# A context loop of VectorE written out, and another order of work at the end of a state space stage

## The reference

```python
# stage D, per batch b and head h: keys and values are the rotated context
scores = jnp.einsum('bhsr,bhlr->bhsl', q_r, k_r)
attn   = jax.nn.softmax(scores, axis=-1)           # over 1601 context tokens
ctx_c  = jnp.einsum('bhsl,bld->bhsd', attn, kv_r)
# stage E, after the state recurrence has given y
y = jnp.moveaxis(ys, 0, 1) + D_param[None, None, :, None] * xs
g = y.reshape(b, l, INTER) * _silu(gate)           # INTER = 2048
g = g * jax.lax.rsqrt(jnp.mean(g * g, axis=-1, keepdims=True) + EPS) * norm_w
return jnp.einsum('bli,di->bld', g, W_out)
```

## Time and profile before

| | us |
|---|---|
| three runs of the kernel | 1403.39, 1405.93, 1405.85 (median 1405.85) |
| the profiled execution, device time | 1405.07 |
| its span, first to last instruction | 1403.2 |
| context loop of stage D, units 0 to 31 | about 575 to 989 |
| pairs and output chunks of stage E | about 1065 to 1237 |
| stage F | from 1237 to the end |

### The profile page before, as it was taken

One profiled execution on the slowest core, in us unless ns is written; L12 is line 12 of the kernel. 1 busy time (PEld: TensorE's weight loads), 2 busy tenths in 40 slices (PEclk: granted clock), 3 DMA queues, 4 the chain that ended last, 5 costly groups with the idle time before them and its releaser, 6 DMA issues.

```text
span 1403.2 us, 23741 instructions
## 1 busy us (share of the span) xinstructions
PE 1354.3 (97%) x8774; PEld 1124.2 (80%) x8774; DVE 983.2 (70%) x1501; ACT 629.8 (45%) x1325; POOL 682.5 (49%) x473
## 2 busy tenths in 40 slices
PE   6999999999999998899999999999999999999998
PEld 4677778778877776899899899999778887767886
DVE  5456676668569998787777787877546777955555
ACT  3534443253343334666566666666325545431000
POOL 3342577678737774441341331500474655626663
PEclk9999999999999999999999999999999999999999
DMA  4121123323232221000000001000132221212231
GB/s 146 49 74 47 61 84 97 90 76 95 78 141 84 87 81 60 1 26 25 1 25 24 1 25 35 19 2 1 58 107 60 76 76 61 91 38 83 91 101 63
DMA packets 30892, 85.63 MB, mean 61 GB/s; under 512 B 3408, under 2 KB 3536, under 8 KB 30544
## 3 DMA queue, kind: packets, MB, share of 16 engines
q1 hardware_dynamic: 30800, 84.43, 19.2%
HBM read 83.37 MB, written 1.05 MB: 60 GB/s over the span
## 4 chain that ended last, share of the span: by engine, by line
PE 76%; DVE 10%; ACT 7%; issue 6%; POOL 0%; DMA 0%; DVEq 0%; ACTq 0%; POOLq 0%
PE psum L904 22%; PE psum L905 21%; PE psum L906 21%; PE psum L1442 3%; DVE part_max L2596 3%; ACT expo L1981 2%; PE psum L932 1%; PE psum L940 1%; ACT expo_t L1988 1%; ACT expo L1976 1%; DVE sq_sum L2826 1%; DVE expo_t L2174 1%; DVE q_pair L2174 1%; PE psum L1635 1%; PE psum L1622 1%
## 5 line engine op out<-in xcount | busy, mean ns | idle before, releaser
L660 POOL TENSOR_SCALAR wpair<-landing 128x1024 fp32r<-128x1024 f32 (+3 forms) x116 | 108.2, 933 | 386.0 <-PE psum L906 258.7
L663 POOL TENSOR_TENSOR wpair<-landing,wpair 128x1024 fp32r<-128x1024 f32 (+3 forms) x116 | 239.3, 2063 | 9.7
L904 PE MATMUL psum<-xn,wpair 128*128 128x512 f32 (+1 forms) x552 | 212.3, 385 | 1.2 <-POOL wpair L663 0.8
L905 PE MATMUL psum<-xn,wpair 128*128 128x512 f32 (+1 forms) x552 | 208.1, 377 | 0.0
L906 PE MATMUL psum<-xn,wpair 128*128 128x512 f32 (+1 forms) x552 | 207.5, 376 | 0.0
L2174 DVE TENSOR_TENSOR expo_t<-psum,expo_t 128x512 fp32r<-128x512 f32 (+1 forms) x224 | 143.5, 651 | 76.7 <-ACT expo_t L1988 69.2
L1988 ACT CAST expo_t<-psum 128x512 fp32r<-128x512 f32 (+1 forms) x224 | 124.3, 565 | 123.8 <-PE psum L1442 123.8
L904 PE MATMUL psum<-expo_t,kv_pair 128*128 128x256 f32 (+1 forms) x416 | 133.7, 321 | 0.2 <-DVE expo_t L2174 0.2
L1442 PE MATMUL psum<-const,expo 128*128 128x128 f32 (+1 forms) x832 | 128.1, 273 | 5.3 <-DVE expo_t L2174 4.6
L2596 DVE TENSOR_REDUCE part_max<-psum 128x1 f32<-128x804 f32 x126 | 121.3, 988 | 6.1 <-PE psum L906 2.1
L761 POOL TENSOR_TENSOR wpair<-landing,wpair 128x512 fp32r<-128x512 f32 x80 | 120.9, 1511 | 6.7
(11 more groups left out here) (326 smaller groups left out, 3285.3 us busy)
## 6 DMA issues: line engine op xcount, KB each, us to landing
landing<-in_weights SPq DMA_DIRECT2D x75, 512.0 KB, 3.6
landing<-in_weights SPq DMA_DIRECT2D x105, 256.0 KB, 2.6
kv<-in_ctx SPq DMA_DIRECT2D x8, 832.0 KB, 4.4
landing<-in_weights SPq DMA_DIRECT2D x15, 320.0 KB, 2.8
rope_k<-in_rope_k SPq DMA_DIRECT2D x1, 1664.0 KB, 7.7
const<-in_constants SPq DMA_DIRECT2D x1, 1184.0 KB, 8.7
x<-in_x SPq DMA_DIRECT2D x4, 256.0 KB, 4.2
out<-x SPq DMA_DIRECT2D x1, 1024.0 KB, 4.3
```

The costliest lines, as they stand in the source:

```text
L660: pool.tensor_scalar(wpair[:, slot, 0, 0:width], landing[:, slot, 0:width], 1.0, 1.0, ALU.mult, ALU.mult).then_inc(chunk_high, 1)
L663: pool.tensor_tensor(wpair[:, slot, 1, 0:width], landing[:, slot, 0:width], wpair[:, slot, 0, 0:width].bitcast(F32), ALU.subtract).then_in ...
L904: pe.matmul(out, w(0), act(0), start=start, stop=False)
L905: pe.matmul(out, w(0), act(1), start=False, stop=False)
```

## The change

Stage D, DVE only: the hardware loop over the first three passes of `units` becomes a Python loop, so that its instructions are written out three times with constants in place of registers. PE and ACT keep their loops.

Stage E: PE now runs `output_chunk(0)` ahead of `turn_inner(7)` and `output_chunk(1)` ahead of `mamba_outputs(7)`. ACT makes the high parts of chunk 0 during pair 7, between `decay_exps(6)` and the first gate Silu, and DVE makes their low parts ahead of `outputs(6)`. From tile 4 on, ACT writes a further full-precision product `norm_w * big` to bank 6 or 7 (`gated_values`), and DVE makes the low part as a tensor_tensor of that bank and the high part. From tile 4 on, squares go to banks 4 and 5 in place of `y_sq`. Squares are made and added one chunk later than the low parts until chunk 6, where two chunks of them follow. `square_means` uses bank 4.

```diff
@@ PE
-                    pe.matmul(bank(6), constant("mean"), sq_sum[:, :], start=True, stop=True).then_inc(norm_sum, 1)
+                    pe.matmul(bank(4), constant("mean"), sq_sum[:, :], start=True, stop=True).then_inc(norm_sum, 1)
...
                 decay_sums(IT // 2 - 1)
-                turn_inner(IT // 2 - 1)
...
-                for c in range(8):
+                output_chunk(0)
+                turn_inner(IT // 2 - 1)
+                output_chunk(1)
+                mamba_outputs(IT // 2 - 1)
+                for c in range(2, 8):
                     output_chunk(c)
-                    if c == 0:
-                        mamba_outputs(IT // 2 - 1)
@@ ACT
+                def gated_values(c):
+
+                    act.wait_ge(mixed, IT)
+                    for kk in range(2):
+                        tile = 2 * c + kk
+                        act.wait_ge(y_gated, tile + 1)
+                        if c > 2:
+                            act.wait_ge(gh_low, tile - 1)
+                        act.activation(bank(6 + kk), gated_tile(tile), ACT.Copy,
+                                       scale=small_at("norm_w")[:, tile:tile + 1]).then_inc(gh_value, 1)
+
+                def gated_squares(c):
+
+                    if c >= 2:
+                        act.wait_ge(y_gated, IT)
+                    for kk in range(2):
+                        tile = 2 * c + kk
                         if tile >= 2:
                             act.wait_ge(sq_added, tile - 1)
-                        act.activation(y_sq[:, kk, :], gated, ACT.Square).then_inc(y_squared, 1)
-
-                for c in range(8):
+                        out = bank(4 + kk) if c >= 2 else y_sq[:, kk, :]
+                        act.activation(out, gated_tile(tile), ACT.Square).then_inc(y_squared, 1)
+
+                for i in range(IT // 2):
+                    inner_in(i)
+                    if i:
+                        decay_exps(i - 1)
+                    if i == IT // 2 - 1:
+                        gated_high(0)
+                    gate_silus(i, 0)
+                    inner_silus(i)
+                    gate_silus(i, 1)
+                decay_exps(IT // 2 - 1)
+                gated_high(1)
+                gated_squares(0)
+                gated_high(2)
+                gated_values(2)
+                gated_squares(1)
+                for c in range(3, 8):
+                    gated_values(c)
                     gated_high(c)
+                    if c < 7:
+                        gated_squares(c - 1)
+                    if c >= 6:
+                        gated_squares(c)
@@ DVE
-                with dve.Fori(0, B // 2 - 1) as i:
+                for i in range(B // 2 - 1):
                     units(i, False)
                 units(B // 2 - 1, True)
...
+                        if c < 2:
+                            dve.scalar_tensor_tensor(out=rest, in0=big[:, T * tile:T * (tile + 1)],
+                                                     scalar=small_at("norm_w")[:, tile:tile + 1], in1=high.bitcast(F32),
+                                                     op0=ALU.mult, op1=ALU.subtract).then_inc(gh_low, 1)
+                        else:
+                            dve.wait_ge(gh_value, tile - 3)
+                            low(rest, bank(6 + kk), high).then_inc(gh_low, 1)
...
-                            dve.tensor_tensor(sq_sum[:, :], sq_sum[:, :], y_sq[:, kk, :], ALU.add).then_inc(sq_added, 1)
-
+                            square = bank(4 + kk) if c >= 2 else y_sq[:, kk, :]
+                            dve.tensor_tensor(sq_sum[:, :], sq_sum[:, :], square, ALU.add).then_inc(sq_added, 1)
+
+                gated_low(0)
                 outputs(IT // 2 - 2)
-                gated_low(0)
+                gated_low(1)
+                squares_added(0)
                 inner_by_dt(IT // 2 - 1)
                 mixes(IT // 2 - 1)
-                squares_added(0)
-                gated_low(1)
+                gated_low(2)
+                squares_added(1)
                 outputs(IT // 2 - 1)
-                squares_added(1)
-                for c in range(2, 8):
+                for c in range(3, 8):
                     gated_low(c)
-                    squares_added(c)
+                    if c < 7:
+                        squares_added(c - 1)
+                    if c >= 6:
+                        squares_added(c)
```

More of the change, by code:

```diff
@@ L528, in perceiver_stack @@
         norm_sum, norm_log, norm_inv = sem("norm_sum"), sem("norm_log"), sem("norm_inv")
-        gh_high, gh_low = sem("gh_high"), sem("gh_low")
+        gh_high, gh_low, gh_value = sem("gh_high"), sem("gh_low"), sem("gh_value")
         e_out, e_scaled = sem("e_out"), sem("e_scaled")
@@ L2115, in gate_silus, with gated_tile @@
                     act.activation(silu_g[:, i % 2, m, :], bank(2 + m), ACT.Silu).then_inc(gate_silu, 1)
-                for i in range(IT // 2):
-                    inner_in(i)
-                    if i:
-                        decay_exps(i - 1)
-                    gate_silus(i, 0)
-                    inner_silus(i)
-                    gate_silus(i, 1)
-                decay_exps(IT // 2 - 1)
+                def gated_tile(tile):
+                    return big[:, T * tile:T * (tile + 1)]
                 def gated_high(c):
@@ L2133, in gated_high @@
                         tile = 2 * c + kk
-                        gated = big[:, T * tile:T * (tile + 1)]
                         act.wait_ge(y_gated, tile + 1)
-                        act.activation(gated_pair[:, 2 * (c % 2) + kk, 0, :], gated, ACT.Copy,
+                        act.activation(gated_pair[:, 2 * (c % 2) + kk, 0, :], gated_tile(tile), ACT.Copy,
                                        scale=small_at("norm_w")[:, tile:tile + 1]).then_inc(gh_high, 1)
+                def gated_values(c):
[7 more added lines that the diff above has]
+                                       scale=small_at("norm_w")[:, tile:tile + 1]).then_inc(gh_value, 1)
@@ L2143, in _ @@
+                gated_squares(1)
+                for c in range(3, 8):
+                    gated_values(c)
                     gated_high(c)
+                    if c < 7:
+                        gated_squares(c - 1)
+                    if c >= 6:
+                        gated_squares(c)
                 act.wait_ge(norm_sum, 1)
-                act.activation(rstd[:, :], bank(6), ACT.Ln, bias=eps[:, 0:1], scale=H / INNER).then_inc(norm_log, 1)
+                act.activation(rstd[:, :], bank(4), ACT.Ln, bias=eps[:, 0:1], scale=H / INNER).then_inc(norm_log, 1)
@@ L2810, in gated_low @@
                         tile = 2 * c + kk
+                        high = gated_pair[:, 2 * (c % 2) + kk, 0, :]
+                        rest = gated_pair[:, 2 * (c % 2) + kk, 1, :]
                         dve.wait_ge(gh_high, tile + 1)
-                        dve.scalar_tensor_tensor(out=gated_pair[:, 2 * (c % 2) + kk, 1, :],
-                                                 in0=big[:, T * tile:T * (tile + 1)],
-                                                 scalar=small_at("norm_w")[:, tile:tile + 1],
-                                                 in1=gated_pair[:, 2 * (c % 2) + kk, 0, :].bitcast(F32),
-                                                 op0=ALU.mult, op1=ALU.subtract).then_inc(gh_low, 1)
+                        if c < 2:
[5 more added lines that the diff above has]
+                            low(rest, bank(6 + kk), high).then_inc(gh_low, 1)
                 def squares_added(c):
```

## The result

The changed kernel takes 1391.3 us (median of four runs, 1390.59 to 1392.25) where the kernel before takes 1405.28 (four runs, 1403.39 to 1405.93): 14.0 us less, a ratio of 0.9897 with a 95% interval of 0.9883 to 0.9911. The forecast was 1392.6. The profiled execution goes from 1405.07 to 1390.59 us.

The account below looks back on a forecast made before the run. PE was taken as the bound, busy for 1354.3 of 1403.2 us, with gains only where it waits or runs slowly. Savings of 6.95 + 6.0 = 12.9 us led to a forecast of 1392.6 us, range 1389.8 to 1399.6.

Parts of the forecast that it names:

- Part 1: Context loop on DVE: writing it out removes two jumps back and saves 6.95 us, bounds 5.8 to 7.2.
- a written-out unit would run like unit 24: Context loop: units 8 and 16 fall from 16.87 and 15.84 to 12.88 us, saving 3.99 and 2.96.
- 1.0 us of unit 8: Context loop: the 1.0 us between the two units' savings is PE's slow stretch, which goes with the wait.
- Part 2: End of stage E: the new order on PE starts `square_means` 6.0 us earlier, bounds 5.0 to 6.5.
- The waits: End of stage E: no new condition delays PE; 1.7 us spare at chunk 3, 1.8 at the last square.
- Rival 1: End of stage E: new waits at chunk 3 or the last square replace the old; 1395.6 to 1396.4 us, chance 0.14.
- Rival 2: Context loop: pauses at page edges, or ACT's and PE's jumps, take its gain; 1399.6 us, chance 0.10.
- Rival 3: Stage D's latent loop falls across a page edge, six jumps at 2.96 us each; slower, 1410.4 us, chance 0.04.
- my own bullet on DVE: End of stage E: low parts with a PSUM operand take 0.69 us, so DVE needs some 2.8 us per chunk, not 5.6.
- The sum: Whole kernel: 6.95 from the loop plus 6.0 from the end of stage E, 12.9 us less.

Follow-up runs that it names:

- loop_only: The kernel before with only DVE's context loop written out, stage E unchanged: 1396.72 us, ratio 0.9942.
- pad8: The kernel before, hardware loop kept, with 8 unread semaphore increments at the start of DVE's program: 1397.25 us, ratio 0.9950.
- pad5: The kernel before, hardware loop kept, with 5 unread semaphore increments at the start of DVE's program: 1397.94 us, ratio 0.9944.
- act_pad95: The changed kernel with 95 unread semaphore increments at the start of ACT's program: 1392.05 us, ratio 0.9903 to the kernel before.
- pad112: The kernel before, hardware loop kept, with 112 unread semaphore increments at the start of DVE's program: 1403.04 us, ratio 0.9978.
- order_now: The kernel before with stage E's new order, operands in SBUF, each chunk's squares made and added at once from chunk 3: 1402.38 us, ratio 0.9977.
- order_only: The kernel before with stage E's new order and lagged squares, operands kept in SBUF, hardware loop kept: 1407.34 us, ratio 1.0012.
- pad4: The kernel before, hardware loop kept, with 4 unread semaphore increments at the start of DVE's program: 1408.30 us, ratio 1.0007.
- end_only: The changed kernel with DVE's hardware loop kept, so only the end of stage E differs from the kernel before: 1398.36 us, ratio 0.9958.
- pad8_end: The changed kernel with DVE's hardware loop kept and shifted by 8 semaphore increments: 1391.67 us, ratio 0.9903 to the kernel before.
- psum_only: The kernel before, old order and hardware loop kept, with values and squares in PSUM from tile 4 on: 1403.43 us, ratio 0.9987.
- psum_now: The changed kernel with each chunk's squares made and added at once from chunk 3 on: 1391.86 us, ratio 0.9906 to the kernel before.

## Why the prediction was right, and where it was not

**Part 1, forecast 6.95, measured 6.97** (loop_only, by the same units). The step that a written-out unit would run like unit 24 held to 0.03 us. I gave as the cause the jump and its fetch; pad8 and pad5 show that it is only half of it. A jump back is free here when the body touches three blocks, and costs 2.65 us and more when it touches four. Writing out is one way past that, and eight increments another.

That 1.0 us of unit 8 is a slow stretch of PE is borne out. Window of the kernel before behind its first pause (us, PE, PEld, DVE, ACT, POOL, PEclk, DMA share, GB/s), then the one behind its second, where unit 16 takes 15.84:

```profile
687.30:690.70 3.40, 3.27 (x13) 2.93 (x12) 2.31 (x5) 2.10 (x7) 0.00 (x0) 0.50 0.00 0
793.00:800.00 7.00, 5.31 (x37) 5.10 (x38) 5.62 (x10) 3.97 (x11) 0.00 (x0) 1.00 0.00 1
```

PE granted 0.50, the lower level (1.2 GHz), for 3.4 us after it had waited. Over all profiles, seven kernels pause at both jumps of DVE (14 units), and 9 of these have such a stretch; the seven that don't pause there (14 units, act_pad95 among them) have none. In the kernels with both pauses, of some 2.7 and 0.6 us, a unit takes 16.69 to 17.07 us with the stretch and 15.84 to 15.89 without. So it was luck that the one execution I had read showed one stretch in two units, close to the 9 in 14 of all: with none in it my sum would have been 1.0 us smaller, with two 1.0 us larger.

**Part 2, forecast 6.0, measured 5.7** (48.06 - 42.4 to L1643; 5.8 to L932). Piece by piece:

| | forecast, us | measured, us |
|---|---|---|
| `decay_sums(7)` to the first product | 0.93 | 1171.61 - 1170.58 = 1.03 |
| chunk 0 | 5.6 | 1177.21 - 1171.61 = 5.60 |
| `turn_inner(7)` | 0.87 | 1178.00 - 1177.21 = 0.79 |
| chunk 1 | 5.6 | 1183.76 - 1178.00 = 5.76 |
| `mamba_outputs(7)` | 1.09 | 1184.86 - 1183.76 = 1.10 |
| chunks 2 to 6 | 28.0 | 1212.95 - 1184.86 = 28.09 |

The terms mis-sized are the change over from L1609 to a product (0.1) and the first product behind the turn and the outputs, whose successor starts 0.77 and 0.80 us later where the pace is 0.70 for three matmuls.

**The waits.** Mapped by the start of L1609 (8.63 us earlier than before), `outputs(7)` was due to end at 1188.0 and ends at 1187.85; the low part of the first tile of chunk 3 was due at 1188.7 and its pair of rows starts at 1187.77 with 0.65 each, so it is there at about 1188.4, some 2.1 us ahead of PE; the last square was due at 1210.9 and ends at 1211.0, 1.95 ahead of L1643 (forecast 1.8). **Rival 1** fell on these. **Rival 2** fell on the issue waits: none is left on DVE in the loop, and the following units are no longer. What I gave for it, a pause of 0.60 us that came without a jump, I had misread: it belongs to the jump, 5 instructions behind it, and goes with it in pad5 and pad8. **Rival 3** didn't come about: the waits of DVE in the latent loop are those of the earlier trace rows:

```profile
DVE lat_pair L2207 <- ACT lat_pair L2053: 23.3, 14, 1.7
```

Its idea, that a shift of the program sets a loop over an edge, is right all the same: act_pad95 does it with ACT's loop, and pad112 puts DVE's over the next edge. What its price left out is that a pause needs a body that touches four blocks, by the table above, and so short a body touches two at most.

**Where the working failed.** I wrote of the shared port pair that it "is not needed for the sum, as PE waited for DVE only at the end". That contradicts my own bullet on DVE, whose 2.8 us per chunk rests on low parts out of PSUM at 0.69 us. Without them the sum is 3.6 us at most and not 6.0 (order_now), and with the change's squares it turns to a loss of 0.8 (order_only). What the profile after shows is DVE's two low parts at 1.30 us while POOL splits, where two from SBUF took 3.55. The Trainium skill (SBUF — State Buffer, SBUF: two separate sides) says that a DVE operation contends with GpSimd's if it has two inputs in SBUF. Low part and square have one there and one in PSUM after the change. The traces agree with this: 3.55 to 3.95 and 1.48 to 4.26 us for two with both in SBUF, 1.30 and 1.47 with one.

**The sum.** 6.97 + 5.78 = 12.8, and 14.0 came (14.5 between the two profiled executions). The rest, 1.2 to 1.7 us, I had no term for. In the two profiles the whole of it lies ahead of the jumps: the kernel after leads by 1.4 us when the loop begins and by 679.05 - 677.43 = 1.62 at the end of unit 7, while the rest of the span from stage F's norm on is as long in both (1403.2 - 1233.46 = 169.74 and 1388.8 - 1219.05 = 169.75) and between the two they differ by the sum, 12.8. No instruction ahead of the jumps is changed, but one stretch at the lower level is 6.8 us in before and 3.4 in after. Window of each:

```profile
547.40:554.20 6.80, 6.80 (x22) 5.61 (x22) 3.19 (x5) 2.48 (x6) 2.44 (x3) 0.50 0.00 0
```
```profile
548.50:551.90 3.40, 3.40 (x11) 2.60 (x10) 1.36 (x3) 1.25 (x3) 1.28 (x1) 0.51 0.00 0
```

3.4 us more at half the pace is 1.7 us. In that place it is 6.8 us in pad112 and pad4 too, 3.4 in nine profiles, that of the changed kernel among them, and absent in order_now and act_pad95, so one profile proves nothing. Over all runs, though, the excess is steady. By the medians loop_only gains 8.6 us where its units explain 7.0, pad5 8.4 against 6.7, end_only 7.0 against 5.8, pad8_end 13.9 against 12.5; psum_only and order_now, with their pauses kept, 2.1 against 1.9 and 3.9 against 3.6. The mean granted clock over the runs goes the same way: 0.993 to 0.994 for the kernel before, 0.995 to 0.997 with one part whole, 0.997 to 0.998 with both. So a kernel with fewer pauses of PE is also granted more clock outside of the places where they were. That is a correlation over these kernels, and why it reaches stretches that come ahead of the change stays open.

It does tell why the parts sum to 15.6. Over the 133 runs of these kernels a straight line, with one slope for all and one base for each kernel, gives 1.1 us of time for each 0.001 of mean granted clock, and what is left scatters by 0.7 us. This is an estimate from the runs' own times and clocks. At equal clock loop_only gains 5.6 us and end_only 4.2, together 9.8, and the kernels with both parts whole gain 9.2 to 10.1 (psum_now, pad8_end and the changed one). So what is saved at equal clock adds up, and what each part brings alone and both bring only once is clock: of the 14.0 us some 4 to 5 are clock, which my sum had in part, as the slow stretches in unit 8 and behind the turn. In the same way loop_only's 8.6 us, by which its rival would stand, are the loop's 7.0 and clock.

## What to carry to other kernels

Where an engine pauses at a loop's jump back with "issue" as the releaser, count the instructions of the body and shift it by a few increments before writing it out: from the second pause one can read how far the next edge is. Give a DVE operation beside a busy GpSimd an operand in PSUM, and don't move its work to the end of a stage unless it is fast there. When two edits are timed together, look also at the distance between two fixed points of PE, as it told 0.1 us here where the medians scatter by 1 to 3.

## What the runs showed of the hardware that I had not expected

- One semaphore increment of DVE, at a distance of half a millisecond from the loop, moves the kernel by 10.4 us (1408.30 to 1397.94). DVE stands idle for 2.56 to 2.89 us at a jump that needs a fetch, 5.00 and 5.03 where two fall together, 0.60 to 0.73 more where the second is 5 instructions on, and nothing more where it is 21 on.
- ACT pauses when its loop is shifted over an edge, too (0.78 and 0.84 us of idle time that the changed kernel has not), and it costs 0.8 us in all.
- While PE works, the lower clock comes in stretches of 3.4 us or twice that. The ones of 3.4 us are worth about 1.0 to 1.7 us each. They come also in code that is the same in every kernel, and fewer of them in kernels in which PE pauses less. The time of a kernel goes with it: order_now took 1400.55 us at a mean granted clock of 0.997 and 1406.37 at 0.992.
- A DVE addition into `sq_sum` takes 0.7 us with a square in PSUM, and up to 2.1 (4.26 for two) with both operands in SBUF beside POOL's split; POOL's own split (L663) takes 2.7 us then and 2.4 in the changed kernel.
